# An audio tower's attention on Trainium2: forward groups of twelve tiles, a ring of five slots, and the residual kept in memory

## What is computed

```
h = token_mixer(x)                               # 8 rounds up and down, (8, 750, 64)
n = layernorm(h)
q, vf, vb = split(n @ wqv.T + b)                 # 8 heads of 64 channels each
k = n[:, :, None, :] * wk
a[s, t, head] = -sum_w |q[s, head, w] - k[t, head, w]| / 8
a = softmax over s (with one more score of 0)
o = sum over heads of (a forwards @ vf  +  a backwards @ vb)
h = h + n + (o * sigmoid(1.702 * o)) @ fanin.T + fanin_b
out = h + mixture_of_8_experts(layernorm(h))     # top 2 by gate
```

## Time and profile before

| | |
|---|---|
| median of three runs | 8943.42 us (8937.65 to 8949.63) |
| the profiled execution | 8950.86 us |
| its span | 8949.1 us |
| TensorE busy | 98% |
| ScalarE busy | 86% |
| VectorE busy | 78% |
| GpSimd busy | 1% |

### The profile page before, as it was taken

One profiled execution on the slowest core, in us unless ns is written; L12 is line 12 of the kernel. 1 busy time (PEld: TensorE's weight loads), 2 busy tenths in 40 slices (PEclk: granted clock), 3 DMA queues, 4 the chain that ended last, 5 costly groups with the idle time before them and its releaser, 6 DMA issues. The chain is left out here.

```text
span 8949.1 us, 255296 instructions
## 1 busy us (share of the span) xinstructions
PE 8741.1 (98%) x115382; PEld 7003.0 (78%) x115382; DVE 6953.8 (78%) x5259; ACT 7728.7 (86%) x3721; POOL 54.9 (1%) x32
## 2 busy tenths in 40 slices
PE   7599999999999999999999999999999999999989
PEld 3279997989948987889968898688857888598863
DVE  3388888888888888888888888888888887888863
ACT  2299999999999999999989999999999999999965
POOL 1000000000000000000000000000000000000000
PEclk9799999999999999999999999999999999999989
DMA  2310000101010010100000010100001010000000
GB/s 79 123 17 2 17 2 2 17 2 17 2 17 2 2 17 2 17 2 17 2 10 8 2 17 2 17 2 17 2 2 17 2 17 2 17 2 2 2 12 8
DMA packets 134892, 114.72 MB, mean 13 GB/s; under 512 B 110954, under 2 KB 114474, under 8 KB 133530
## 3 DMA queue, kind: packets, MB, share of 16 engines
q1 hardware_dynamic: 133792, 98.00, 5.3%
HBM read 57.74 MB, written 40.22 MB: 11 GB/s over the span
## 5 line engine op out<-in xcount | busy, mean ns | idle before, releaser
L749 PE MATMUL sc<-ring,window 128*32 128x375 f32 x96000 | 7966.4, 478 | 1.7 <-DVE ring L870 1.7
L800 ACT ACTIVATE ring<-qx,xs 128x3000 f32<-128x3000 f32 x2624 | 7178.1, 2792 | 727.1 <-PE sc L749 726.2
L870 DVE TENSOR_SCALAR ring<-qx,xs 128x3000 f32<-128x3000 f32 x3376 | 6131.3, 1837 | 1478.9 <-PE sc L749 1405.0
L749 PEld LDWEIGHTS sc<-ring,window 128*32 128x32 f32 x96000 | 6124.6, 109 | 1306.6 <-issue 389.8
L722 PEld LDWEIGHTS acc<-ext,vf 128*32 128x32 f32 x9408 | 362.5, 109 | 38.2 <-issue 9.9
L709 PE MATMUL acc<-ex,vb 128*32 128x375 f32 x3088 | 382.9, 478 | 1.5 <-DVE ex L827 1.5
L722 PE MATMUL acc<-ext,vf 128*32 128x128 f32 (+1 forms) x9408 | 374.6, 270 | 0.2 <-DVE ext L835 0.2
L835 DVE STREAM_TRANSPOSE ext<-ex 128x768 f32<-128x768 f32 x385 | 374.1, 972 | 0.6
L785 ACT ACTIVATE ex<-sc 128x750 f32<-128x750 f32 x385 | 299.1, 777 | 5.6 <-PE sc L749 5.6
L738 PE MATMUL sc<-ksum,select 128*32 128x375 bf16 x3072 | 261.0, 324 | 33.8 <-DMA vf<-scratch_v 17.6
L738 PEld LDWEIGHTS sc<-ksum,select 128*32 128x32 bf16 x3072 | 187.1, 95 | 91.4 <-issue 33.8
(11 more groups left out here) (179 smaller groups left out, 1021.8 us busy)
## 6 DMA issues: line engine op xcount, KB each, us to landing
scratch_v<-vs SPq DMA_DIRECT2D x24, 1000.0 KB
qx<-scratch_qk SPq DMA_DIRECT2D x64, 375.0 KB
scratch_qk<-qs SPq DMA_DIRECT2D x32, 375.0 KB, 14.2
vb<-scratch_v SPq DMA_DIRECT2D x128, 92.0 KB
vf<-scratch_v SPq DMA_DIRECT2D x64, 184.0 KB
xs<-scratch_x SPq DMA_DIRECT2D x16, 187.5 KB
vb<-scratch_v SPq DMA_DIRECT2D x128, 1.8 KB
scratch_x<-xt SPq DMA_DIRECT2D x1, 1500.0 KB, 5.0
```

Of the source, the lines that this page charges most:

```text
L749: mm = pe.matmul(bank[32 * j:32 * j + 32, h, 0:HALF], window[:, HALF_NH * g + j, ROWS - 1 - i:3 * ROWS - 1 - i], ring[:, slot, j, h * HALF ...
L800: act.activation(flat(ring[:, (HALF * g + k) % RING, :, :]), flat(qx[g][:, :, :]), ACT.Abs, bias=xs[g][:, 1, k:k + 1], scale=0.5).then_inc ...
L870: vec.tensor_scalar(flat(ring[:, (HALF * g + k) % RING, :, :]), flat(qx[g][:, :, :]), xs[g][:, 0, k:k + 1], xs[g][:, 1, k:k + 1], ALU.max, ...
```

## The change

GROUP goes from 8 to 12, so a pair has NG = 2 forward groups (of 192 and 183 columns) instead of 3 (of 128, 128 and 119), and there are 33 groups in all where there were 49. Each `ext` grows by half, from 24,576 to 36,864 bytes in each partition. To make room, RING goes from 6 to 5 (a slot is 12,000 bytes), and `hx` (12,000 bytes) is no longer held through attention: SP stores it to a new scratch tensor in memory, behind the value stores of the second sequence, and loads it again at the start of the last phase, where VectorE waits for it (`h_in`) before its first product. The waits that count groups are written with NG.

```diff
-GROUP = 8
+GROUP = 12
-RING = 6
+RING = 5
...
+    scratch_h = nc.dram_tensor("scratch_h", (128, TC), F32, kind="Internal").ap()
...
-        hx = sbuf(whole, "hx", [128, B, HALF])
...
+            hx = sbuf(inner, "hx", [128, TC])
+            h_made = semaphore(inner, "h_made")
+            h_stored = semaphore(inner, "h_stored")
...
+                        if b == 1:
+                            sp.wait_ge(h_made, 1)
+                            sp.dma_start(scratch_h, hx[:, :]).then_inc(h_stored, 16)
...
                     sp.wait_ge(xs_stored, 16)
+                    sp.wait_ge(h_stored, 16)
...
-                    pool.tensor_tensor(hx[:, :, :].rearrange("p b l -> p (b l)"), ht[:, :], xt[:, :], ALU.add)
+                    pool.tensor_tensor(hx[:, :], ht[:, :], xt[:, :], ALU.add).then_inc(h_made, 1)
...
                     if t % GROUP == 0:
-                        vec.wait_ge(group_done, n * NG + (t // GROUP + 3))
+                        vec.wait_ge(group_done, n * NG + (t // GROUP + NG))
...
-                    vec.wait_ge(group_done, n * NG + 4)
+                    vec.wait_ge(group_done, n * NG + (NG + 1))
...
+        hx = sbuf(ctx, "hx_d", [128, TC])
...
                     sp.dma_start(avg[:, :], A["avg"]).then_inc(w_first, 16)
+                    sp.dma_start(hx[:, :], scratch_h).then_inc(h_in, 16)
                     sp.dma_start(wgt[:, :], A["wgt"]).then_inc(w_gate, 16)
...
                     vec.wait_ge(w_first, 48)
+                    vec.wait_ge(h_in, 16)
```

More of the change, by code:

```diff
@@ L78, in build, with phase_tokens @@
         select = sbuf(whole, "select", [128, 128], BF16)
-        phase_tokens(nc, A, sbuf, psum, semaphore, hx, oacc, window, select, scratch_x, scratch_qk, scratch_ks, scratch_v)
+        phase_tokens(nc, A, sbuf, psum, semaphore, oacc, window, select, scratch_h, scratch_x, scratch_qk, scratch_ks, scratch_v)
         phase_attend(nc, sbuf, psum, semaphore, oacc, window, select, scratch_x, scratch_qk, scratch_ks, scratch_v)
-        phase_feed(nc, A, out, sbuf, psum, semaphore, hx, oacc)
-def phase_tokens(nc, A, sbuf, psum, semaphore, hx, oacc, window, select, scratch_x, scratch_qk, scratch_ks, scratch_v):
+        phase_feed(nc, A, out, sbuf, psum, semaphore, scratch_h, oacc)
+def phase_tokens(nc, A, sbuf, psum, semaphore, oacc, window, select, scratch_h, scratch_x, scratch_qk, scratch_ks, scratch_v):
     with ExitStack() as ctx:
@@ L894, in _, with phase_feed @@
                 keep(NPAIR, 1, B)
-def phase_feed(nc, A, out, sbuf, psum, semaphore, hx, oacc):
+def phase_feed(nc, A, out, sbuf, psum, semaphore, scratch_h, oacc):
     with ExitStack() as ctx:
+        hx = sbuf(ctx, "hx_d", [128, TC])
         h2 = sbuf(ctx, "h2", [128, TC])
@@ L912, in phase_feed @@
         comb = sbuf(ctx, "comb", [CH, NCC, 2, NE])
+        h_in = semaphore(ctx, "h_in")
         w_first = semaphore(ctx, "w_first")
@@ L1276, in _ @@
                     flat = oacc[:, 1:, :].rearrange("p b l -> p (b l)")
-                    hflat = hx[:, :, :].rearrange("p b l -> p (b l)")
                     def link(ins):
@@ L1291, in added @@
                         vec.wait_ge(y_sum, c + 1)
-                        vec.scalar_tensor_tensor(h2[:, cols(c)], py[:, c % 2, 0:EC], fbc[:, 0:1], hflat[:, cols(c)],
+                        vec.scalar_tensor_tensor(h2[:, cols(c)], py[:, c % 2, 0:EC], fbc[:, 0:1], hx[:, cols(c)],
                                                  ALU.add, ALU.add).then_inc(h_made, 1)
```

## The result

| | before | changed |
|---|---|---|
| median, 16 runs of each | 8946.35 us | 8962.98 us |
| ratio | | 1.0018, 95% interval 1.0011 to 1.0025 |
| the profiled execution's span | 8949.1 us | 8961.4 us |

The changed kernel is 16.6 us (0.18%) slower. The forecast was +14.6 us, a median of 8958.0 in a range from 8941 to 8980, with "the same" (within about 0.2%) the likeliest. The point and the range held; the parts of the sum did not all hold, and two of its errors cancelled, which was luck. To see that I cut each trace at the same five places: xt's store, the first clear, TensorE's first matmul of attention, its first tile, and SP's first issue of the last phase.

The account below looks back on a forecast made before the run. TensorE, busy for 98% of the span, was taken to bound attention. Terms −1 + 2.6 + 2.6 + 5.9 + 2 + 2.5 gave +14.6 us, a median of 8958.0 us, in a range from 8941 to 8980.

Parts of the forecast that it names:

- −1 us for 3072 fewer MATMULs: Attention's forward blocks on TensorE: same columns in fewer instructions save only the cost beside columns, −0.3 to −1.3 us.
- +2.6 for the wider empty group: First pair's forward group, run on zeroes: 192 MATMULs of 183 columns instead of 119 add 2.6 us on TensorE.
- bound of 0.4 ns beside the columns: TensorE in attention: an instruction costs at most 0.4 ns besides its columns, read from tile times.
- The ring of five, +2 us: Ring slots in attention: no loss inside tiles, 0 to 0.4 us at each of 15 pair ends, +2 us taken.
- row 1 at 2983.3 (0.3 us late): At a pair's end, VectorE's row 1 of the next pair is done 0.3 us after TensorE wants it.
- Rival A: Ring decides at pair starts: full 1.26 us lost at 15 places, 19 us, total +31.6, 8975 us; chance 0.22.
- The clear, +2.6 us: Before attention, VectorE clears 9216 elements of the turned buffer instead of 6144, uncovered: +2.6 us.
- The store, +5.9 us: Projections, SP's queue: storing the residual's 1500 KB behind the second sequence's value stores adds 5.9 us, 0 to 9.0.
- The load, +2.5 us: Last phase's start: the residual's load ahead of four small loads delays TensorE's first matmul by 2.5 us, +1.5 to +6.6.
- placed behind 1500 KB it lands at about 8650.9: Last phase's start: `ident` lands at about 8650.9 behind the residual's load, where TensorE began at 8648.35 before: +2.5 us.
- Rival B: Residual's memory traffic is hidden, store in queue gaps, load mostly behind small ones: +5 to +8, 8950 us; chance 0.20.
- Rival C: Wider groups pay in attention because blocks cost more than their columns: −20, 8923 us; chance 0.05.

Follow-up runs that it names:

- the early store: Changed kernel with the residual stored right behind xt, ahead of the first query stores: 8959.3 us, 1.0014 of before.
- the run with the clear alone: Kernel before with only the turned buffer's clear moved from VectorE to GpSimd: 8942.0 us against 8946.9 (0.9994).

## Why the prediction was right or wrong

**Columns, not instructions.** Right in the mechanism, low in the small term. The forecast took −1 us for 3072 fewer MATMULs and +2.6 for the wider empty group, and the tiles have the same price a column at 96, 128 and 192 columns. Its bound of 0.4 ns beside the columns was too tight: the pairs show 0.5 to 0.9, which makes −1.5 to −2.8 us. The +2.6 can be seen at the other end, in the drain that grows by as much: from the last pair's start to SP's first issue it is 521.9 to 522.1 us with groups of eight and 524.3 to 524.6 with twelve. With groups of six, whose drain is narrower still, it is 522.0 where columns alone would give 520.7; single pairs scatter by as much. The 2.5 ns for each matmul, which the Trainium skill states (TensorE: Matmul & The Clock Gate, "Wait — 56ns, not 53.3ns?") and the prediction weighed against the rows, would have been an estimated −7.7 us; the pairs disagree with it here. Attention is 8231.2, 8233.4, 8232.4, 8232.8 and 8234.1 us with groups of twelve, and 8232.1, 8232.9, 8230.5 and 8230.8 with eight and six slots: means 8232.8 and 8231.6, +1.2 us, with a scatter as large.

**The ring of five, +2 us.** The mechanism was there: the chain at a pair's end moved by 1.14 us (forecast 1.3), and row 1 has no slack left. The stall was not. The step that failed is "row 1 at 2983.3 (0.3 us late)", and my taking 2 us for it: the row is on time, and a weight load's short wait is hidden. Groups of eight with five and with six slots (8231.3 and 8232.9 us of attention; 7192.5 and 7191.8 to 7194.1 for the 14 pairs) bound the cost below the scatter. Rival A, and its 19 us, is refuted. Inside a tile the reading held too: with three slots the waits come that it describes.

**The clear, +2.6 us.** Right: 7.74 us against 5.18. Another 0.6 us, of waiting in front of it, was not in the sum.

**The store, +5.9 us.** Right: 4.6 us in this pair of traces, 5.7 as a mean. That it is a full queue's price, and nothing in a gap, was shown by the early store. How much of it is a fixed cost of a store (the forecast took 2.4 us of it for that) no run shows.

**The load, +2.5 us.** Mis-sized. The step that failed is "placed behind 1500 KB it lands at about 8650.9", with its upper bound of +6.6 from the slowest load. It took the landing of a store of the same size, in an empty queue (5.0 us; 8643.89 + 5.0 is 8648.9, and the 8649.3 written there counts from the end of the issue), and put `ident` 1.6 us behind it, which is about the time between their issues and leaves no room for anything that holds a small load up. The residual landed after 6.6 us, and `ident` came 4.8 us behind the residual: while it was on its way the DMA engines were busy for 0.95 and then 0.85, where it had been 0.53. That the small load shares them with the 1500 KB in front and with the 2 MB behind (the experts' weights for the most part) is my reading; before, the 2 MB alone left it at 3.2 us. The first matmul came 6.9 us later, past the upper bound, and the last phase is 312.5 us as a mean of six kernels with the load there, +5.9 on before's 306.6 and +7.2 on the 305.3 of the run with the clear alone.

**The sum** came out by luck: attention was taken 4.5 us too long and the last phase 4.8 us too short in the traces compared. Rival B (the traffic is hidden) did not happen, but could have been had: with both transfers moved it costs nothing. Rival C fell with the tiles.

## What to carry to other kernels

Before merging matmuls, divide the length of a block by its columns at both widths in the trace: where the price is the same, wider instructions buy next to nothing (1.3 us in 7193 here, within the scatter), and the weight loads' busy time on the page says nothing about it. A buffer that is spilled to make room costs what its place in the queue costs: the same 1500 KB were 5.7 us in a full queue and nothing in a gap, and the load was 6 us in front of a small one that TensorE waited for, and nothing behind it. A ring can be judged by hand: a row's slot comes free, then release and production, against the rows in between.

## What the runs showed of the hardware that I had not expected

- A 64 KB load with 1500 KB in front of it and 2 MB behind landed 9.6 us after its issue (3.2 us without the 1500 KB).
- With four array columns working together, forward MATMULs of 96 columns follow each other every 20.0 ns.
- GpSimd clears float32 as fast as VectorE: 9216 elements in 128 partitions in 7.78 and 7.74 us.
- A VectorE subtraction of 0.67 us took 4.26 us beside a GpSimd subtraction of 4.06 us.
